# Attention probabilities transposed by DMA in place of TensorE, in a deeper pipeline, with TensorE's attention steps as a loop

## The reference

```python
x = x + tanh(g_xattn[0]) * attention(layernorm(x), ctx_512, ...)   # 16 heads, latent keys and values with rope
x = x + tanh(g_ffn[0]) * ffn(layernorm(x), ...)                    # shared MLP plus 8 routed experts, top 2
```

## Time and profile before

| | |
|---|---|
| median of 3 runs (lowest, highest) | 2038.41 us (2034.86, 2039.94) |
| the profiled execution, its own time | 2040.83 us |
| its span | 2039.0 us |
| TensorE busy | 1962.0 us, 96% |
| VectorE, ScalarE, GpSimd busy | 954.1, 673.9, 569.5 us |
| mean busy share of the DMA engines, by queue | 33.8% (SP's), 6.6% (GpSimd's) |

### The profile page before, as it was taken

One profiled execution on the slowest core, in us unless ns is written; L12 is line 12 of the kernel. 1 busy time (PEld: TensorE's weight loads), 2 busy tenths in 40 slices (PEclk: granted clock), 3 DMA queues, 4 the chain that ended last, 5 costly groups with the idle time before them and its releaser, 6 DMA issues.

```text
span 2039.0 us, 32958 instructions
## 1 busy us (share of the span) xinstructions
PE 1962.0 (96%) x12313; PEld 1122.1 (55%) x12484; DVE 954.1 (47%) x1947; ACT 673.9 (33%) x1905; POOL 569.5 (28%) x651
## 2 busy tenths in 40 slices
PE   7799999999999999879999999999999999999999
PEld 7466666666666666444445555555554444444444
DVE  5666666666666665546633222222223423233243
ACT  4555555555555566521012222222210000000000
POOL 4533333333333354300022433433303110110101
PEclk9899999999999999999999999999999999999999
DMA  9212222222222232141328999989953521221202
GB/s 291 82 50 60 65 61 60 60 60 60 66 65 60 76 117 60 37 127 39 105 59 187 229 252 213 218 217 218 210 115 123 113 75 42 83 83 26 78 16 88
DMA packets 292134, 216.49 MB, mean 106 GB/s; under 512 B 225200, under 2 KB 231088, under 8 KB 292016
## 3 DMA queue, kind: packets, MB, share of 16 engines
q1 hardware_dynamic: 280496, 177.04, 33.8%
q0 software_dynamic: 11520, 37.76, 6.6%
HBM read 113.02 MB, written 48.23 MB: 79 GB/s over the span
## 4 chain that ended last, share of the span: by engine, by line
PE 88%; DVE 5%; ACT 2%; issue 2%; POOL 1%; DMA 1%; SPq 1%; DVEq 0%; POOLq 0%; ACTq 0%
PE o L575 15%; PE score L724 11%; PE p_bank L631 8%; PE o L809 8%; PE score L798 7%; PE o L735 5%; PE p_bank L724 5%; PE m_bank L724 5%; PE c_bank L588 4%; PE p_bank L798 4%; PE m_bank L798 4%; DVE arena L1005 3%; PE c_bank L735 3%; PE t_bank L735 3%; PE score L609 2%
## 5 line engine op out<-in xcount | busy, mean ns | idle before, releaser
L575 PE MATMUL o<-arena 128*128 128x512 bf16 x1473 | 341.0, 381 | 22.0 <-DVE arena L1005 18.4
L575 PEld LDWEIGHTS o<-arena 128*128 128x128 bf16 x1536 | 146.4, 99 | 183.5 <-DVE arena L1005 28.8
L1368 POOL TENSOR_TENSOR arena<-arena 128x512 f32<-128x512 f32 x128 | 133.3, 1042 | 395.1 <-DVE arena L1021 393.4
L849 ACT ACTIVATE arena<-score,arena 128x128 f32<-128x128 f32 x512 | 180.9, 365 | 175.4 <-DVE arena L1045 175.4
L724 PE MATMUL score<-arena 128*128 128x512 bf16 x1036 | 233.7, 379 | 1.1
L631 PE MATMUL p_bank<-arena 128*128 128x256 bf16 x1536 | 182.4, 276 | 0.0
L724 PEld LDWEIGHTS score<-arena 128*128 128x128 bf16 x1056 | 103.3, 98 | 124.3
L1005 DVE TENSOR_TENSOR arena<-arena 128x512 bf16<-128x512 f32 (+2 forms) x219 | 153.2, 709 | 23.1 <-ACT arena L904 8.6
L809 PE MATMUL o<-arena 128*128 128x512 bf16 (+1 forms) x681 | 160.0, 379 | 2.1
L631 PEld LDWEIGHTS p_bank<-arena 128*128 128x128 bf16 x1536 | 147.3, 99 | 25.1 <-issue 0.7
L798 PE MATMUL score<-arena 128*128 128x352 bf16 x960 | 151.5, 315 | 2.9 <-issue 2.9
(11 more groups left out here) (162 smaller groups left out, 2929.5 us busy)
## 6 DMA issues: line engine op xcount, KB each, us to landing
xrow_d<-arena SPq DMA_DIRECT2D x80, 256.0 KB, 3.6
arena<-w_expert SPq DMA_DIRECT2D x32, 544.0 KB, 5.2
arena<-w_shared SPq DMA_DIRECT2D x22, 384.0 KB, 3.5
arena<-x SPq DMA_DIRECT2D x16, 512.0 KB, 4.5
arena<-x SPq DMA_DIRECT2D x32, 256.0 KB, 2.8
x_d<-arena SPq DMA_DIRECT2D x32, 256.0 KB, 2.2
xn_d<-arena SPq DMA_DIRECT2D x32, 256.0 KB, 2.2
arena<-x_d SPq DMA_DIRECT2D x8, 1024.0 KB, 5.7
```

What stands on the lines that cost most here:

```text
L575: mm = pe.matmul(o_bank[b % 2][:, :], lhsT=cT[:, a, h, :], rhs=M_w[:, w, head_of(hg, h), :], start=(hg == 0 and n == 0), stop=(hg == 3 and ...
L849: mm = act.activation(prob[:, u % 4, h, :], score_bank[u % 2][:, h * S:(h + 1) * S], ACT.Exp, bias=neg_max[:, u % 4, h:h + 1], accum_out=d ...
L1368: pool.tensor_tensor(prob[:, u % 4], prob[:, u % 4], rden[:, u % 4, :].unsqueeze(2).broadcast_to([P, 4, S]), ALU.mult).then_inc(normed, 1)
```

## The change

The probabilities are no longer transposed on TensorE. ScalarE casts them in SBUF into a tile `share` (HI), GpSimd subtracts for LO, and SP issues one DMA transpose a unit that brings both into `pT`, now with four buffers. The context is computed two steps ahead of its output instead of one, alternately into `c_bank` and `t_bank`, and `cT` has two buffers. Scores, row maximum, exponentials and reciprocals come two steps earlier. In odd steps ScalarE and VectorE do the exponentials and the row maximum ahead of the context's cast and subtraction, and ScalarE's piece cast comes last. `x1` has four buffers and its loads are a group earlier. The loads and splits of the shared weights take every second step. TensorE's attention goes through `run_steps`, as the other engines' does. The diff, only its changed lines:

```diff
@@ -124,17 +124,18 @@
-        pT_region = words(512)
-        pT = halves(pT_region).rearrange("p (l n) -> p l n", l=2)
-        cT_region = words(512)
-        cT = halves(cT_region).rearrange("p (l h n) -> p l h n", l=2, h=4)
+        cT_region = [words(512) for _ in range(2)]
+        cT = [halves(r).rearrange("p (l h n) -> p l h n", l=2, h=4) for r in cT_region]
+        share = [halves(k_region[:, 4096 + i * 512:4608 + i * 512]).rearrange("p (l n) -> p l n", l=2) for i in range(2)]
+        pT = [halves(k_region[:, 5120 + i * 512:5632 + i * 512]).rearrange("p (l n) -> p l n", l=2) for i in range(4)]
...
-        x1 = words(2 * D).rearrange("p (b n) -> p b n", b=2)
+        x1_region = words(2 * D)
+        x1 = [r[:, i * D:(i + 1) * D] for r in (x1_region, k_region[:, 7168:8192]) for i in range(2)]
@@ -155,7 +156,7 @@
-        assert pT_region.shape == cT_region.shape
+        assert cT_region[0].shape == cT_region[1].shape
@@ -217,8 +218,9 @@
-            return score_bank[1] if q % 2 == 1 and q < 8 else p_bank
...
+            return score_bank[1] if q % 2 == 1 and q < 6 else p_bank
...
+        ctx_bank = [c_bank, t_bank]
@@ -248,7 +250,7 @@
-        pt_mm, pt_hi, pt_lo = sem("pt_mm"), sem("pt_hi"), sem("pt_lo")
+        share_hi, share_lo, pT_in = sem("share_hi"), sem("share_lo"), [sem(f"pT_in{i}") for i in range(4)]
@@ -352,6 +354,13 @@
+                u = k + 3
+                if within(u, NU):
+                    wait(sp, share_lo, u + 1, 16, it)
+                    if it is not None:
+                        sp.sem_inc(turn_begun, 1)
+                    sp.dma_start_transpose(pT[u % 4].rearrange("p l (h n) -> p (l h) n", h=4),
+                                           share[u % 2].rearrange("p l n -> p (l n)")).then_inc(pT_in[u % 4], 16)
@@ -365,7 +374,7 @@
-                    sp.dma_start(x1_d[at(b, 4, it)], x1[:, b % 2, :]).then_inc(x1_out[b % 2], 16)
+                    sp.dma_start(x1_d[at(b, 4, it)], x1[b % 4]).then_inc(x1_out[b % 2], 16)
@@ -383,11 +392,11 @@
-                    for b in (2 * g + 2, 2 * g + 3):
+                    for b in (2 * g + 4, 2 * g + 5):
...
-                            wait(sp, x1_out[b % 2], 16 * (b // 2), 32, it)
-                            wait(sp, xn2_ready, b - 1, 4, it)
-                            sp.dma_start(x1[:, b % 2, :], x[at(b, 4, it)]).then_inc(xres_in[b % 2], 16)
+                            wait(sp, x1_out[b % 2], 16 * (b // 2 - 1), 32, it)
+                            wait(sp, xn2_ready, b - 3, 4, it)
+                            sp.dma_start(x1[b % 4], x[at(b, 4, it)]).then_inc(xres_in[b % 2], 16)
@@ -397,8 +406,8 @@
-                if it is None and within(k - FFN_FIRST + 1, 12):
-                    load_wsh(k - FFN_FIRST + 1)
+                if it is None and (k - FFN_FIRST) % 2 == 1 and within((k - FFN_FIRST + 1) // 2, 12):
+                    load_wsh((k - FFN_FIRST + 1) // 2)
@@ -572,34 +581,27 @@
-                            mm = pe.matmul(o_bank[b % 2][:, :], lhsT=cT[:, a, h, :], rhs=M_w[:, w, head_of(hg, h), :],
+                            mm = pe.matmul(o_bank[b % 2][:, :], lhsT=cT[u % 2][:, a, h, :], rhs=M_w[:, w, head_of(hg, h), :],
...
-                u = k + 1
+                u = k + 2
...
-                    wait(pe, pt_lo, u + 1, 16, it)
-                    wait(pe, ct_lo, u, 16, it)
+                    wait(pe, pT_in[u % 4], 16 * (u // 4 + 1), 64, it)
+                    wait(pe, ct_lo, u - 1, 16, it)
...
-                        mm = pe.matmul(c_bank[:, :], lhsT=kvN[g % 2][:, a, b % 2, :], rhs=pT[:, w, :],
+                        mm = pe.matmul(ctx_bank[u % 2][:, :], lhsT=kvN[g % 2][:, a, b % 2, :], rhs=pT[u % 4][:, w, :],
...
-                u = k + 2
-                if within(u, NU):
-                    wait(pe, normed, u + 1, 16, it)
-                    wait(pe, pt_lo, u, 16, it)
-                    for h in range(4):
-                        mm = pe.transpose(t_bank[:, h * S:(h + 1) * S], prob[:, u % 4, h, :], ident_sb)
-                    mm.then_inc(pt_mm, 1)
-                u = k + 4
+                u = k + 6
...
-                    wait(pe, pr_lo, 8 if u == 0 else 8 * g + 2 * hg + 4, 16, it)
+                    wait(pe, pr_lo, 6 if u == 0 else 8 * g + 2 * hg + 4, 16, it)
@@ -612,7 +614,7 @@
-                    wait(pe, pr_lo, q if q >= 8 else q - 1, 16, it)
+                    wait(pe, pr_lo, q if q >= 6 else q - 1, 16, it)
@@ -741,8 +743,7 @@
-            for k in range(-12, NU):
-                step(k, None)
+            run_steps(pe, step, NU - 1)
@@ -832,25 +833,21 @@
-                u = k + 1
+                u = k + 4
+                if within(u, NU):
+                    wait(act, normed, u + 1, 16, it)
+                    wait(act, pT_in[(u - 2) % 4], 16 * ((u - 2) // 4 + 1), 64, it)
+                    act.copy(share[u % 2][:, HI, :], prob[:, u % 4].rearrange("p h n -> p (h n)"))\
+                        .then_inc(share_hi, 1)
+                if k % 2 == 1:
+                    exps(k + 6, it)
+                u = k + 2
...
-                    act.copy(cT[:, HI].rearrange("p h n -> p (h n)"), c_bank[:, :]).then_inc(ct_hi, 1)
-                u = k + 2
-                if within(u, NU):
-                    wait(act, pt_mm, u + 1, 16, it)
-                    act.copy(pT[:, HI, :], t_bank[:, :]).then_inc(pt_hi, 1)
-                if k % 2 == 1:
-                    upper_piece(k + 12, it)
-                u = k + 4
-                if within(u, NU):
-                    wait(act, maxed, u + 1, 16, it)
-                    for h in range(4):
-                        mm = act.activation(prob[:, u % 4, h, :], score_bank[u % 2][:, h * S:(h + 1) * S], ACT.Exp,
-                                            bias=neg_max[:, u % 4, h:h + 1], accum_out=den[:, u % 4, h:h + 1])
-                    mm.then_inc(exped, 1)
+                    act.copy(cT[u % 2][:, HI].rearrange("p h n -> p (h n)"), ctx_bank[u % 2][:, :]).then_inc(ct_hi, 1)
...
-                    upper_piece(k + 12, it)
+                    exps(k + 6, it)
+                upper_piece(k + 12, it)
@@ -880,8 +877,16 @@
-                if it is None and within(k - FFN_FIRST, 12):
-                    split_wsh(k - FFN_FIRST)
+                if it is None and (k - FFN_FIRST) % 2 == 0 and within((k - FFN_FIRST) // 2, 12):
+                    split_wsh((k - FFN_FIRST) // 2)
...
+            def exps(u, it):
+                if within(u, NU):
+                    wait(act, maxed, u + 1, 16, it)
+                    for h in range(4):
+                        mm = act.activation(prob[:, u % 4, h, :], score_bank[u % 2][:, h * S:(h + 1) * S], ACT.Exp,
+                                            bias=neg_max[:, u % 4, h:h + 1], accum_out=den[:, u % 4, h:h + 1])
+                    mm.then_inc(exped, 1)
@@ -1015,7 +1020,7 @@
-                u = k + 3
+                u = k + 5
@@ -1026,24 +1031,19 @@
-                    dve.scalar_tensor_tensor(out=x1[:, b % 2, :], in0=o_bank[b % 2][:, :], scalar=tanh_sb[:, 0:1],
-                                             in1=x1[:, b % 2, :], op0=ALU.mult, op1=ALU.add).then_inc(x1_done, 1)
-                u = k + 1
+                    dve.scalar_tensor_tensor(out=x1[b % 4], in0=o_bank[b % 2][:, :], scalar=tanh_sb[:, 0:1],
+                                             in1=x1[b % 4], op0=ALU.mult, op1=ALU.add).then_inc(x1_done, 1)
+                if k % 2 == 1:
+                    row_max(k + 6, it)
+                u = k + 2
...
-                    lower(cT[:, LO].rearrange("p h n -> p (h n)"), c_bank[:, :],
-                          cT[:, HI].rearrange("p h n -> p (h n)")).then_inc(ct_lo, 1)
+                    lower(cT[u % 2][:, LO].rearrange("p h n -> p (h n)"), ctx_bank[u % 2][:, :],
+                          cT[u % 2][:, HI].rearrange("p h n -> p (h n)")).then_inc(ct_lo, 1)
...
-                u = k + 2
-                if within(u, NU):
-                    wait(dve, pt_hi, u + 1, 16, it)
-                    lower(pT[:, LO, :], t_bank[:, :], pT[:, HI, :]).then_inc(pt_lo, 1)
+                if k % 2 == 0:
+                    row_max(k + 6, it)
...
-                u = k + 4
-                if within(u, NU):
-                    wait(dve, scored, u // 2 + 1, 8, it)
-                    dve.tensor_reduce(neg_max[:, u % 4, :], score_bank[u % 2][:, :].rearrange("p (h n) -> p h n", h=4),
-                                      AX.X, ALU.max, negate=True).then_inc(maxed, 1)
@@ -1067,12 +1067,18 @@
-                    dve.bn_stats(stats[:, b % 2, :], x1[:, b % 2, :]).then_inc(stat2, 1)
+                    dve.bn_stats(stats[:, b % 2, :], x1[b % 4]).then_inc(stat2, 1)
...
+            def row_max(u, it):
+                if within(u, NU):
+                    wait(dve, scored, u // 2 + 1, 8, it)
+                    dve.tensor_reduce(neg_max[:, u % 4, :], score_bank[u % 2][:, :].rearrange("p (h n) -> p h n", h=4),
```

(15 more changed lines are left out.)

## The result

The changed kernel takes 2052.45 us (median of 4 runs, 2049.54 to 2054.1), against 2036.63 for the kernel before (4 runs, 2034.63 to 2039.94). The ratio is 1.0075, 95% interval 1.0055 to 1.0094: slower by more than the 0.3% that a measurement here can tell. The forecast was 1989, 1952 to 2014. The profiled execution took 2049.54 us with a span of 2047.7 (before 2040.83 and 2039.0).

A forecast was written before the change was run, and what follows sets the result against it. TensorE's work per step plus a small wait was taken as the bound. Attention turns -36.0, last twelve steps -14.6, loop +1.5 us sum to -49.1 on a span of 2039.0, giving 1989 us as a median, range 1952 to 2014.

The forecast's parts named there:

- the stall of 2.3 us a turn: TensorE's waits in each eight-step attention turn, summed from 1.5, 0.3 and 0.5 us; placed between 0 and 4.78.
- (d): No difference, 2038 us: attention stalls near 5.7 us a turn, or transposed tiles landing near 10.6 us late; chance 0.04.
- (c): Eight new GpSimd operations each hold VectorE 0.84 us through the SBUF port: about 2079 us; chance 0.11 with other slower ends.
- 1.5 in the step that closes a batch: Stall a turn, in us, because VectorE frees the key and query pieces' shared bank 1.7 us late.
- 0.3 at the even pieces before it: Smaller TensorE stalls, in us a turn, at the even-step pieces before the batch-closing step.
- The walk that I had written out by hand: VectorE's serial work, with ScalarE's part, over the two steps before the batch-closing one: 7.4 and 5.5, together 12.9 us.
- 0.5 for the port: Stall, in us a turn, where new GpSimd operations hold VectorE's short operations through the SBUF port on the tight stretch.
- the last twelve steps: End of the attention stage, steps without a piece: from 60.6 to 46.0 us, a gain of 14.6 (8 to 16.7).
- Transposes: Probability transposes leaving TensorE save 4.78 us per eight-step attention turn of 49.53, if nothing else comes to bind.
- The loop: TensorE's attention code as a loop: six places between 0 and 2.9 us, taken at 0.3 each, 1.5 us in all.
- rival (b): TensorE's attention loop refills at each jump, 2.9 us each: 2005 us, or 2022 with larger stalls; chance 0.10.
- DMA transposes: Probability transposes on SP's queue, 5.1 us to land, 3.4 us a unit against steps of 3.9 to 6.7: hidden, no cost.

The follow-up runs named there:

- the tenth run: Changed kernel with the old order of odd steps and GpSimd's new subtraction over only 16 of 512 columns: 1961.23 us, ratio 0.962.
- The fourth run: Changed kernel with two of the four key pieces of a group put in another bank, `m_bank`: 2070.57 us, ratio 1.0156.
- the second run: Changed kernel with GpSimd's new subtraction over 16 of 512 columns, the rest of the lower half zero: 2009.11 us, ratio 0.9864.
- the third run: Changed kernel with VectorE's short layernorm operations ahead of its wait for the context's cast in a turn's second step: 2032.35 us, ratio 0.9971.
- the fifth run: Changed kernel with ScalarE's and VectorE's odd steps back in the order of the kernel before: 1981.89 us, ratio 0.9731.
- the seventh run: Changed kernel with, in odd steps, the piece's cast ahead of the exponentials and its subtraction ahead of the context's, context left late: 2024.0 us, ratio 0.9937.
- the ninth: Changed kernel with the old order of odd steps, except that ScalarE casts the piece behind the exponentials: 2049.01 us, ratio 1.0052.
- the first run: Changed kernel with TensorE's attention program as straight code instead of a loop: 2051.85 us, ratio 1.0076.
- the sixth run: Changed kernel with every DMA transpose of the probabilities issued twice, the second after the first has landed: 2085.1 us, ratio 1.024.
- The twelfth run: Changed kernel with the old order of odd steps and ScalarE's cast of the probabilities moved behind the exponentials: 2037.75 us, ratio 0.9993.

## Why the prediction was wrong

**What failed is one term: the stall of 2.3 us a turn.** It was 4.92 us in listed waits, 5.4 by the turns (50.46 against 45.02 in the tenth run) and 5.8 on the mean of steps 0 to 115 (739.4 / 14.54 = 50.85). A turn of 50.85 instead of the forecast 47.05 makes 55 us over 14.54 turns, of the 58 by which the span of 2047.7 misses the forecast 1989.9 (2039.0 - 49.1). The stall lies just above the break-even of 5.7 that the prediction had worked out, and the time came out between (d)'s 2038 and (c)'s 2079. By its parts, which overlap, since a hold lengthens the same walk that the waits hang on:

- *1.5 in the step that closes a batch.* Right in place and nearly in size: 1.80. I had put it at the piece, for the bank; it stands at the scores, which read the key piece of the step before. The fourth run shows that: with another bank the stop stays.
- *0.3 at the even pieces before it.* 0.41 + 2.71 measured, at the third step of the turn. The walk that I had written out by hand is the right one, with the exponentials and the context's cast in it. From the subtraction of the last piece to the release of the key piece it had 0.5 + 0.68 + 1.4 + 0.6 + 0.69 + 0.9 + 0.69 = 5.46 us. It measured 8.03 (410.29 to 418.32), and began 2.46 us behind TensorE's step in place of 2.0. The short operations are what is too small: 0.5 + 0.9 in the sum, 2.26 + 1.66 = 3.92 in the trace. The other terms hold within 0.1.
- *0.5 for the port.* This is the number that failed. The three holds on this one walk are 3 x 0.84 = 2.5 us; without them its short operations would take the 1.4 that I had. The prediction had the length of a hold right, 0.84 us (and 0.16 against 1.02 here), and that PSUM subtractions are not hit (0.69 here). It did not set the holds against the short operations one by one, and left out the multiplication's, which the kernel before has too. With the new subtraction short, the waits of this step fall from 3.12 to 1.3 us (the second run) and a turn by 2.5 us; with the short operations in VectorE's idle time the 2.71 falls to 1.0 (the third run). (The 2.5 holds also what the higher clock gave.) The Trainium skill (SBUF — State Buffer, Who interferes with whom) calls this an exclusive lock; the traces agree, each held operation ending with GpSimd's. That rule as I applied it for rival (c), every hold on the path, would have given 6.7 us a turn; measured 2.5 with the new order and 1.4 with the old. So (c)'s mechanism is there, at less than half its price.

**The order of the odd steps is what puts this walk in TensorE's way.** Shown by the fifth run: with the old order, all else of the change kept, the kernel takes 1981.89 us, 57 faster than before, with the holds still in it. By its steps: steps 0 to 115 take 671.5 us (46.18 a turn), the last twelve 52.6, step 0 starts at 94.45. That 1989 lies so near to this kernel's time is in part luck: the turn is 0.87 us shorter than the 47.05 forecast, the last twelve steps 6.6 us longer. The two halves of the order don't add up: piece early alone 28 us (the seventh run), context early alone 3 (the ninth, no more than the noise), both 70.6. Either half alone leaves one of VectorE's two subtractions of the odd step waiting for a cast that stands behind the exponentials. So the loss has two parts: the order makes the walk about as long as the time that TensorE leaves for it, and the holds make it longer. With the new order taken back, or the new subtraction's holds made short, the kernel was faster than before (1981.89 and 2009.11 us).

**What was right.** *Transposes*: a turn of 45.02 us in the tenth run, where TensorE hardly waits; the prediction had 49.53 - 4.78 = 44.75. *The loop*: put at 1.5 us, 0.6 measured and not told from nothing (the first run), so rival (b) is out. The Trainium skill (Runtime: NRT & Kernel Launch, Instruction fetch mechanics) would have a taken branch to code no longer held cost a fetch; no run here shows one. *DMA transposes*: hidden but for 0.62 us before one context; another 0.92 stands before a query piece. The landing was 3.1 us where I took 5.1 from the expert stage, yet the sixth run shows that the room is small. *The start*: 2.6 us earlier, inside the 3 allowed. A slip without effect: GpSimd's 18.1 us a turn should be 18.0.

**The last twelve steps** gained 7.6, not 14.6: 53.0 against 46.0. The trace has 4.8 us of waits there: 1.55 on GpSimd's value splits, 1.26 on ScalarE, 1.0 and 0.33 on VectorE, 0.62 on a transpose. One group of output matmuls ran 4.44 in place of 2.75 us (below). I had left all of these out. The old order does not mend this part: 52.6 in the fifth run.

**Left open**: whether the hold of the port could be had away by another place for GpSimd's subtraction, with the output kept whole. The twelfth run moved it and lost 56 us, and the cause of that loss was not found.

## What to carry to other kernels

When a change moves an operation in an engine's order, walk each engine's program for every step of the period and write the wait of each operation beside it; the sum of its busy times hides the idle time that lies in it (VectorE was busy 58% of the stretch and still set the pace). Write beside each short operation, too, what GpSimd does at that time: here three VectorE operations of 0.16 us took 1.0 each. In this kernel the operations whose results free a shared buffer belong ahead of the serial group of row maximum and exponentials, and both of them, since one alone gave 28 or 3 us and the two together 70.6. If a relief moves a stop to another place, as in the third, fourth and seventh runs, the chain is the bound and not the buffer.

## What the runs showed of the hardware

**TensorE's clock falls after some of these stops.** The same wait of 2.71 us was followed by 24 matmuls in 2.79 us in one turn (418.38, above) and in 5.30 in the one before:

```profile
366.69 5.30 PE L633 MATMUL p_bank<-arena 128*128 128x256 bf16 x24 [2.71 <-DVE arena L1010]
```

Busy time by stretch around it gives a mean granted clock of 0.57 of full speed, near the lower of its two levels (1.2 and 2.4 GHz):

```profile
365.00:373.00 8.00, 6.09 (x27) 4.13 (x29) 5.20 (x12) 2.52 (x11) 1.83 (x2) 0.57 0.38 98
```

It happened in 8 of 15 turns (4.10 to 5.30 us), and cost less than it seems. A turn with 5.30 took 51.70 us (363.13 to 414.83) and one with 4.46 took 50.52 (515.75 to 566.27), against 50.46 at full clock, since the later stop of 1.80 shrank to 0.33 to 0.66. The seventh run has the same: 12 output matmuls in 4.44 us behind its wait of 2.39. Between 200 and 700 the third, fifth and tenth runs, whose waits there are 1.8 us or less, have no such group; the second has one, 24 matmuls in 4.21 us (266.86) behind waits of 1.79 and 0.94. In the last twelve steps of the changed kernel 12 output matmuls took 4.44 us (856.63) behind waits of 0.62 and 1.26 with a few matmuls between. So the length of the last wait alone doesn't tell whether the clock falls.

**A narrow GpSimd operation frees VectorE sooner.** Over 16 columns it takes 0.22 us in place of 1.16, and VectorE's short operations at that place are back at 0.16. The multiplication behind it still holds one for 1.01 (the second run).
